# Splitting fp32 weight products into fp16 parts in the MLP and QKV projections of a fused transformer kernel

## The chip, the cores and the metric

The kernel runs on one core of a Trainium2 chip. Its time is the device time of one execution in microseconds (us). The engines are TensorE (PE in the profile, with PEld for its weight loads), VectorE (DVE), ScalarE (ACT), GpSimd (POOL) and SyncE (SP, which here only starts transfers).

## What is computed

A batch of 64 images of 224 x 224 with three channels (196 patches of 16 x 16) and 64 texts of 32 tokens. The sequence has 228 tokens of width 256. The reference, cut to what matters:

```python
patches = _patchify(x, 16)                              # 64 x 196 x 768
h = silu(patches @ tok_W1 + b1) @ tok_W2 + b2           # token projection
h = concatenate([h, txt], axis=1)                       # 64 x 228 x 256
# attention block on a = layernorm(h), 16 heads of 16
xn = rms_norm(a, ln1_w)
q, k, v = xn @ Wq, xn @ Wk, xn @ Wv                     # 256 x 256 each
q, k = q / |q|, k / |k|
p = softmax((q k^T + bias) * scale, earlier tokens only)
y = (p v) @ Wo + a
z = relu(rms_norm(y, ln2_w) @ W1) @ W2                  # 256 x 1024, 1024 x 256
h = h + z + y
# expert block on layernorm(h): 8 experts, each takes its best 3648 rows
scores = softmax(ln(h) @ Wr);  G, idx = top_k(scores.T, k)
X_e = gelu(X[idx] @ fW1 + fb1) @ fW2 + fb2
out = h + scatter_add(G * X_e)
```

## The kernel before

The kernel has two phases. In the first, 32 pairs of sequences (PAIRS, two sequences of 228 tokens, as four tiles of T = 114 rows, W = 456 columns when transposed) go through token projection, attention and MLP. The second does the routing and the experts; its products are already done in fp16 parts.

**Pipeline.** An iteration i of the first phase's loop does, on TensorE: the second token product of pair i (`pe_tok2`), the end of the attention of pair i-1, the router product of pair i-2 (`pe_x2T`, `pe_logits`), the output projection (`pe_yT`, `pe_wo`), the transposes of y (`pe_y2T`), and three up-projection blocks of pair i-1 (`pe_w1`; EARLY = 3 of MC = 8). Then come the transposes of pair i's normalised input (`pe_xsT`), one more block, the query, key and value products of pair i (`pe_qkv`, four query and key blocks and two value blocks), the last four up-projection blocks, and the attention of pair i (`pe_attention`). The down-projection of pair i-1 (`pe_w2`) is cut into 16 pieces of two products each: two pieces stand ahead of the transposed keys (`pe_qkT`), four between the first of them, and ten in numbered slots between the score and value products of the 16 groups of heads (`SLOTS`). The first token product of pair i+1 fills later slots. Iterations 1 to 30 are of this kind; the last (31) has no next token product, and a part "last" finishes the MLP of the last pair.

**Banks.** All products but the scores and the value products go through two PSUM banks, G[0] and G[1]. `BANKED`, `body` and `ORDER` write down by hand in which order blocks use each bank; a block may start when the one before it in its bank is evacuated (`wait_free`). All eight transposed query-key blocks use G[1].

**Other engines.** ScalarE evacuates the transposes (`act_evacuate`), the hidden blocks (`relu`), the queries and keys, and takes the exponentials (`exps`). VectorE does the layer norm and the normalised inputs xs and xa (`front_b`), the norms of queries and keys (`qk_norm`: a sum of squares for each of four tiles, a reciprocal root in 13 small steps, a scaling, and the fp16 low parts, after which the keys may be transposed), the multiplication with the bias table (`masked_probs`, 16 a pair), and the MLP output added to the residual (`mlp_out` after groups 1 and 6, `mlp_stats` after 7). POOL computes small norms, copies the high parts of queries, computes xn2 (`second_norm`), and reorders the images (`turn_images`), which SP then spreads over partitions (`spread_images`). Each engine works through its own list strictly in order.

**Start.** SP's queue loads the token weights and the images, spreads the first pair, loads the second, then the small weights; it writes the bias table to DRAM (`zrow_d`) when VectorE has made it, loads it back in eight transfers, then the attention and MLP weights, and only then spreads the second pair's images. POOL's list has the copy for the second pair's images ahead of the high parts of pair 0.

## Time and profile before

| | |
|---|---|
| median of 3 runs | 4300.19 us (4299.0 to 4302.61) |
| profiled execution | 4297.36 us, span 4295.6 us |
| granted TensorE clock, mean of the span | 0.968 |
| TensorE matmul busy | 3876.5 us, 90% |
| VectorE busy | 2403.7 us, 56% |
| ScalarE busy | 2035.7 us, 47% |
| GpSimd busy | 1716.9 us, 40% |

Busy shares are averages over both phases. In a timeline row a run of like instructions is merged: its start, its length, the engine, the line, the operation, output<-input, the shapes and the count, and in brackets how long the engine was idle before it and what ended that. Ends of matmuls include the time in which results drain, so the next row can start before the end of the one above. An fp32 product shows as two instructions.

### The profile page before, as it was taken

How to read it: one execution, taken by the hardware profiler on the slowest of the kernel's cores; microseconds unless marked ns; L12 is line 12 of the kernel's file. 1: busy time of each engine (PE TensorE's matmuls, PEld its weight loads, DVE VectorE, ACT ScalarE, POOL GpSimd, SP SyncE). 2: the span in 40 equal slices, each digit the busy share in tenths (PEclk: the TensorE clock that was granted, in tenths of full speed). 3: DMA queues.
4: the chain of work that ended last, by engine and by line, in shares of the span. 5: the costliest groups of instructions: out<-in, count | busy, mean ns of one | idle time of the engine just before them, and what ended most of it. 6: DMA issues, size and time to landing. Idle time of an engine off the chain costs nothing. (4 is left out here: it accounts for less than half of the span.)

```text
span 4295.6 us, 78024 instructions
## 1 busy us (share of the span) xinstructions
PE 3876.5 (90%) x26650; PEld 2354.5 (55%) x26650; DVE 2403.7 (56%) x4812; ACT 2035.7 (47%) x3375; POOL 1716.9 (40%) x1367
## 2 busy tenths in 40 slices
PE   2699999999999999999999999339999999999998
PEld 1366566566566566566566566235555555555554
DVE  3455555555555555555555555475555555555554
ACT  1344444444444444444444444225665655655565
POOL 1123323323323323323323322016666666666666
PEclk8799999999999999999999999659999999999999
DMA  7412312312312312312312310532323323323322
GB/s 113 87 35 43 49 34 44 49 34 44 49 34 44 49 34 44 49 34 44 49 34 44 49 22 16 143 99 39 63 45 66 63 46 65 65 46 66 46 46 45
DMA packets 302872, 222.26 MB, mean 52 GB/s; under 512 B 111524, under 2 KB 290182, under 8 KB 302710
## 3 DMA queue, kind: packets, MB, share of 16 engines
q1 hardware_dynamic: 183550, 157.86, 19.1%
q0 software_dynamic: 107264, 62.29, 9.3%
q10 hardware_dynamic: 11896, 0.05, 0.2%
q8 instruction: 89, 1.46, 0.1%
q14 instruction: 73, 0.60, 0.0%
HBM read 117.43 MB, written 63.57 MB: 42 GB/s over the span
## 5 line engine op out<-in xcount | busy, mean ns | idle before, releaser
L1382 DVE TENSOR_TENSOR pr<-pr,bias_t 114x684 f32<-114x684 f32 x512 | 485.6, 968 | 166.3 <-ACT pr L1018 161.9
L1729 POOL DMA_INDIRECT out_dram<-contrib,idx_cur x256 | 531.5, 2076 | 104.8 <-issue 78.8
L1558 DVE SCALAR_TENSOR_TENSOR hTs<-hTe,scales,hTs 128x456 f16<-128x456 f32 x514 | 322.4, 686 | 445.5 <-ACT hTs L1132 445.5
L1018 ACT ACTIVATE pr<-SC 114x684 f32<-114x684 f32 x512 | 376.5, 743 | 339.7 <-PE SC L445 339.4
L511 PE MATMUL G<-w2m,hT 128*114 128x256 f32 x2048 | 511.4, 388 | 1.1 <-DVE hy L1354 1.1
L891 PE MATMUL SC<-xgT,ws 128*128 128x456 f16 x2316 | 468.4, 357 | 0.0
L1722 POOL DMA_INDIRECT xg<-xn_rows,idx_cur x264 | 389.9, 1477 | 117.1 <-issue 60.4
L493 PE MATMUL G<-yT,w1m 128*128 128x456 f32 x1024 | 412.2, 551 | 10.6 <-ACT yT L964 10.6
L371 PE MATMUL G<-img,w1t 128*128 128x392 f32 x768 | 343.4, 538 | 68.3 <-DMA b2t<-in_L_tok_b_dram 49.9
L511 PEld LDWEIGHTS G<-w2m,hT 128*114 128x114 f32 x2048 | 339.9, 178 | 75.6 <-ACT hT L1054 15.4
L1660 POOL TENSOR_TENSOR rstd<-mv,ln_eps 114x4 f32<-114x4 f32 x32 | 7.0, 220 | 881.0 <-DVE mv L1255 881.0
L891 PEld LDWEIGHTS SC<-xgT,ws 128*128 128x128 f16 x2316 | 227.1, 98 | 220.3 <-issue 2.2
L1132 ACT ACTIVATE hTs<-hTe,scales 128x456 f16<-128x456 f32 x514 | 330.7, 670 | 0.0
L1125 ACT ACTIVATE hTe<-SC,fb1c,unscales 128x456 f32<-128x456 f32 x386 | 280.8, 728 | 54.4 <-PE SC L891 54.3
L902 PE MATMUL Y<-hTs,ws 128*128 128x456 f16 x1536 | 306.3, 356 | 0.0
L902 PE MATMUL SC<-hTs,ws 128*128 128x456 f16 x1536 | 306.3, 356 | 0.0
L493 PEld LDWEIGHTS G<-yT,w1m 128*128 128x128 f32 x1024 | 189.4, 190 | 180.5 <-issue 154.8
L1324 DVE COPY qkT<-G 128x912 f16<-128x912 f16 x128 | 81.0, 633 | 341.5 <-PE G L426 341.5
L1676 POOL CAST qkp<-qkraw 114x256 f16<-114x256 f32 x128 | 90.4, 744 | 444.6 <-DVE qkraw L1311 444.6
L1684 POOL COPY turned<-raw 96x1568 f32<-96x1568 f32 x64 | 203.3, 3176 | 114.6 <-DMA img<-turned 67.8
L1293 DVE TENSOR_TENSOR sqb<-qkraw 114x512 f32<-114x512 f32 x128 | 88.6, 692 | 277.9 <-ACT qkraw L964 277.9
L426 PE MATMUL G<-ident_h,qkp 114*128 114x114 f16 x2048 | 148.5, 216 | 93.5 <-POOL qkp L1676 48.7
(229 smaller groups left out, 6725.3 us busy)
## 6 DMA issues: line engine op xcount, KB each, us to landing
raw<-in_x_dram SPq DMA_DIRECT2D x192, 196.0 KB, 6.4
img<-turned SPq DMA_DIRECT2D x384, 98.0 KB, 2.8
we<-in_L_ffn_W_dram SPq DMA_DIRECT2D x34, 1024.0 KB, 7.7
out_dram<-hy SPq DMA_DIRECT2D x32, 456.0 KB
xn_rows<-xn SPq DMA_DIRECT2D x32, 456.0 KB
xg<-xn_rows,idx_cur POOLq DMA_INDIRECT x264, 3.8
out_dram<-contrib,idx_cur POOLq DMA_INDIRECT x256, 5.5
bias_by_distance<-pr SPq DMA_DIRECT2D x1, 3241.9 KB, 37.9
```

Source lines behind the costliest of these rows:

```text
L371: last = pe.matmul(part.g(*key)[:, 0:2 * NP_], w1t[:, k, m * 128:(m + 1) * 128], img[:, k, :, :].rearrange("p b n -> p (b n)"), start=k == ...
L493: last = pe.matmul(part.g("w1", m)[:, 0:W], w1m[:, c, m * 128:(m + 1) * 128], yT[:, c, :], start=c == 0, stop=c == KC - 1)
L511: last = pe.matmul(part.g("w2", b)[0:T, at:at + D], hT[:, m, t * T:(t + 1) * T], w2m[:, m, :], start=m == 0, stop=m == MC - 1)
L891: last = pe.matmul(RING[bank2(key)][:, 0:W], ws1[eb][:, wp, c, m * 128:(m + 1) * 128], xgT[:, xp, c, :], start=c == 0 and i == 0, stop=c = ...
L902: last = pe.matmul(RING[bank2(key)][:, 0:W], ws2[eb][:, wp, m, c * 128:(c + 1) * 128], hTs[:, hp, m, :], start=m == 0 and i == 0, stop=m = ...
L1018: act.activation(pr[g % 4][:, :, :], SC[g % 2][0:T, :, 0:QW], ACT.Exp).then_inc(exp_done, 1)
L1125: act.activation(hTe[:, m, :], RING[bank2(key)][:, 0:W], ACT.Gelu, bias=bias[:, at:at + 1] if isinstance(at, int) else bias[:, bass.ds(at, ...
L1132: act.activation(hTs[:, 0, m, :], hTe[:, m, :], ACT.Identity, scale=scale_at(scales, 2, e)).then_inc(h_high, 1)
L1382: dve.tensor_tensor(pr[g % 4][:, :, :], pr[g % 4][:, :, :], bias_t[:, 2 * pair:2 * pair + 2, :], ALU.mult).then_inc(probs_done, 1)
L1558: dve.scalar_tensor_tensor(hTs[:, 1, m, :], hTe[:, m, :], scale_at(scales, 2, e), hTs[:, 0, m, :], ALU.mult, ALU.subtract).then_inc(h_spli ...
L1722: pool.indirect_dma_start(out=xg[k4][:, t, :], out_offset=None, in_=xd[:, :], in_offset=bass.IndirectOffsetOnAxis(ap=idx_cur[k4][:, t:t + ...
L1729: pool.indirect_dma_start(out=out_rows, out_offset=bass.IndirectOffsetOnAxis(ap=idx_cur[k4][:, t:t + 1], axis=0), in_=contrib[k][:, t, :], ...
```

## The change

Six edits, all in the first phase.

- **Operands in two fp16 parts.** The weights of QKV, up- and down-projection are kept as a high part (rounded to fp16 after scaling by a power of two) and a low part (what is left); so are the transposed inputs and the hidden layer. A product becomes three fp16 products: high x high, high x low, low x high. `wo`, the token weights and the router stay fp32.
- **Evacuation in two passes.** ScalarE writes the high part from PSUM (`xs_high`, `y2_high`, `hid_high`); VectorE then reads the same PSUM block and the high part and writes the low part (`xs_low`, `y2_low`, `hid_low`); only then is the bank free. Evacuations of queries, keys and values take a scale.
- **Order.** All eight up-projection blocks stand ahead of QKV. Of the 16 down-projection pieces 12 stand ahead of the first transposed keys, two behind it, one each in slots 0 and 2. `mlp_out` for the first two tiles is moved into `qk_norm`, between the scaling and the low parts, the other two behind group 4, the statistics behind group 5.
- **Preparing weights.** The QKV weights are squared, scaled and split between the first token product and the first QKV (`qkv_split`); the MLP weights between the first attention and iteration 1 (`mlp_split_weights`). The raw weights lie in buffers that are used otherwise later.
- **Start.** The bias table waits for its own three small loads only and is written before the first images are spread, 341 columns instead of 455; it comes back in two transfers and one broadcast, and its subtraction stands before `qk_norm`. The expert biases are loaded on SP's queue after the second pair's images.
- **End.** For the last pair VectorE computes xn2 instead of POOL, and ScalarE does all eight hidden blocks.

```diff
-        wqkv = s1("wqkv", [128, KC, 3 * D])
+        wqkv = s1("wqkv", [128, 2, KC, 3 * D], F16)
-        w1m = s1("w1m", [128, KC, HID])
-        w2m = s1("w2m", [128, MC, D])
+        w1m = s1("w1m", [128, 2, KC, HID], F16)
+        w2m = s1("w2m", [128, 2, MC, D], F16)
...
         body = (
-            [("tok2", 0)] + BANKED["after"][0] + w1_blocks(0, 0, EARLY) + BANKED["front"][0] + BANKED["qkv"][0]
-            + w1_blocks(0, EARLY, MC) + [("w2", 0), ("w2", 1)],
+            [("tok2", 0)] + BANKED["after"][0] + w1_blocks(0, 0, EARLY) + BANKED["front"][0] + w1_blocks(0, EARLY, MC)
+            + BANKED["qkv"][0] + [("w2", 0), ("w2", 1)],
...
+        PARTS = ((0, 0), (0, 1), (1, 0))
...
                     for c in range(KC):
-                        last = pe.matmul(part.g(*key)[0:T, :], xsT[:, c, t * T:(t + 1) * T], wqkv[:, c, 0:2 * D],
-                                         start=c == 0, stop=c == KC - 1)
+                        for n, (wp, xp) in enumerate(PARTS):
+                            last = pe.matmul(part.g(*key)[0:T, :], xh[:, xp, c, t * T:(t + 1) * T], wqkv[:, wp, c, 0:2 * D],
+                                             start=c == 0 and n == 0, stop=c == KC - 1 and n == len(PARTS) - 1)
...
-                last = pe.matmul(part.g("w1", m)[:, 0:W], w1m[:, c, m * 128:(m + 1) * 128], yT[:, c, :],
-                                 start=c == 0, stop=c == KC - 1)
+                for n, (wp, yp) in enumerate(PARTS):
+                    last = pe.matmul(part.g("w1", m)[:, 0:W], w1m[:, wp, c, m * 128:(m + 1) * 128], yh[:, yp, c, :],
+                                     start=c == 0 and n == 0, stop=c == KC - 1 and n == len(PARTS) - 1)
...
-                    last = pe.matmul(part.g("w2", b)[0:T, at:at + D], hT[:, m, t * T:(t + 1) * T], w2m[:, m, :],
-                                     start=m == 0, stop=m == MC - 1)
+                    for i, (wp, hp) in enumerate(PARTS):
+                        last = pe.matmul(part.g("w2", b)[0:T, at:at + D], hT[:, hp, m, t * T:(t + 1) * T], w2m[:, wp, m, :],
+                                         start=m == 0 and i == 0, stop=m == MC - 1 and i == len(PARTS) - 1)
...
-        for n, slot in enumerate((0, 1, 4, 4, 5, 6, 7, 8, 9, 10)):
-            SLOTS[slot].append(("w2", range(6 + n, 7 + n)))
+        for n, slot in enumerate((0, 2)):
+            SLOTS[slot].append(("w2", range(14 + n, 15 + n)))
...
-            w2(0)
+            for n in range(0, 12, 2):
+                w2(n)
             pe_qkT(part, j, 0)
-            w2(2)
+            w2(12)
             pe_qkT(part, j, 1)
             pe_scores(part, j, 0, first)
-            w2(4)
             pe_scores(part, j, 1, first)
...
                 pe_xsT(part, i)
-                pe_w1(part, EARLY)
+                for m in range(EARLY, MC):
+                    pe_w1(part, m)
                 pe_qkv(part, i)
-                for m in range(EARLY + 1, MC):
-                    pe_w1(part, m)
                 pe_attention(part, i)
...
-                    act.activation(hT[:, m, :], part.g("w1", m)[:, 0:W], ACT.Relu).then_inc(evacuated[part.bank("w1", m)], 1)
+                    act.activation(hT[:, 0, m, :], part.g("w1", m)[:, 0:W], ACT.Relu).then_inc(hid_high, 1)
...
+            flat = lambda t: t.rearrange("p c n -> p (c n)")
+            squares_of(wo[:, :, :], yT[:, :, 0:D], WO_SUM, mlp_squares)
+            squares_of(flat(w1m_raw), words(w1m), W1_SUM, mlp_squares)
+            squares_of(flat(w2m_raw), words(w2m), W2_SUM, mlp_squares)
+            act.wait_ge(mlp_scale, 1)
+            high_weights(w1m[:, 0, :, :], w1m_raw, W1_K, mlp_high)
+            high_weights(w2m[:, 0, :, :], w2m_raw, W2_K, mlp_high)
...
                 xs_transposed(part)
-                relu(part, [EARLY])
+                relu(part, range(EARLY, MC))
                 queries_keys(part, i)
-                relu(part, range(EARLY + 1, MC - 2))
-                high_parts(i, range(3))
-                relu(part, [MC - 2])
-                high_parts(i, range(3, NT))
-                relu(part, [MC - 1])
+                high_parts(i, range(NT))
                 exps(part, i)
...
+            def hid_low(part, j, ms):
+                for m in ms:
+                    dve.wait_ge(hid_high, MC * j + (m + 1))
+                    dve.scalar_tensor_tensor(hT[:, 1, m, :], part.g("w1", m)[:, 0:W], 0.0, hT[:, 0, m, :],
+                                             ALU.max, ALU.subtract).then_inc(evacuated[part.bank("w1", m)], 1)
...
+                if part.kind != "first":
+                    mlp_out(part, j - 1, 0)
                 for t in range(NT):
                     dve.wait_ge(qk_high, NT * j + (t + 1))
...
                 router_out(i - 2)
-                front_b(part, i)
+                front_xs(i, range(2))
+                y2_low(part, i - 1)
+                front_xs(i, range(2, NT)).then_inc(xs_done, 1)
+                hid_low(part, i - 1, range(EARLY))
+                xs_low(part, i)
+                hid_low(part, i - 1, range(EARLY, MC))
+                front_xa(part, i)
                 qk_norm(part, i)
                 masked_probs(part, i)
```

## Rows read from the trace of the kernel before

**Rows 1.** The page's first part: busy time, share and instructions of each engine.

```profile
PE 3876.5 (90%) x26650; PEld 2354.5 (55%) x26650; DVE 2403.7 (56%) x4812; ACT 2035.7 (47%) x3375; POOL 1716.9 (40%) x1367
```

**Rows 2.** Windows: length; busy PE, PEld, DVE, ACT, POOL; PEclk; DMA share; GB/s.

```profile
64.10:66.80 2.70, 0.04 (x1) 0.00 (x0) 2.50 (x10) 0.00 (x0) 0.00 (x0) 1.00 0.92 98
67.00:72.00 5.00, 0.00 (x0) 0.00 (x0) 1.51 (x3) 0.00 (x0) 3.95 (x8) 0.50 0.94 99
...
137.00:148.70 11.70, 8.55 (x88) 5.98 (x89) 3.70 (x5) 5.68 (x8) 0.00 (x0) 0.50 1.00 139
149.00:155.50 6.50, 3.87 (x58) 2.27 (x55) 5.00 (x5) 3.66 (x6) 2.86 (x1) 1.00 0.31 35
155.80:159.00 3.20, 3.20 (x30) 1.50 (x28) 1.40 (x2) 0.00 (x0) 0.00 (x0) 0.50 0.00 0
...
1464.40:1545.00 80.60, 76.74 (x569) 48.26 (x569) 46.90 (x100) 36.36 (x63) 24.22 (x24) 1.00 0.24 42
...
2656.00:2667.50 11.50, 6.96 (x153) 4.83 (x153) 9.42 (x20) 6.22 (x11) 9.08 (x6) 1.00 0.14 43
```

**Rows 3.** Timeline of PE over one body iteration.

```profile
1464.42 1.95 PE L389 MATMUL G<-w2t,hid 128*114 128x256 f32 x8
...
1476.66 1.00 PE L360 MATMUL G<-ident,yn 114*128 114x114 f32 x8 [0.78 <-DVE yn L1372]
...
1485.52 7.03 PE L406 MATMUL G<-wqkv,xsT 128*114 128x512 f32 x16
...
1495.84 6.28 PE L493 MATMUL G<-yT,w1m 128*128 128x456 f32 x16
1501.96 1.91 PE L511 MATMUL G<-w2m,hT 128*114 128x256 f32 x8
1505.28 0.57 PE L426 MATMUL G<-ident_h,qkp 114*128 114x114 f16 x8 [1.42 <-DVE qkp L1319]
...
1545.00 1.95 PE L389 MATMUL G<-w2t,hid 128*114 128x256 f32 x8
```

**Rows 4.** Timelines of ACT and DVE in the same iteration.

```profile
1481.32 0.55 ACT L1054 ACTIVATE hT<-G 128x456 f32<-128x456 f32 x1 [0.98 <-PE G L493]
...
1478.86 1.37 DVE L1286 TENSOR_SCALAR xa<-h,mv,lt 114x256 f32<-114x256 f32 x4
...
1494.65 0.23 DVE L1301 TENSOR_SCALAR ss<-ss 114x128 f32<-114x128 f32 x1
...
1498.63 2.90 DVE L1311 TENSOR_TENSOR qkraw<-qkraw,rn 114x512 f32<-114x512 f32 x4
1501.45 1.15 DVE L1318 TENSOR_TENSOR qkp<-qkraw,qkp 114x256 f16<-114x256 f32 x2
```

**Rows 5.** Groups of instructions: busy us, mean ns of one, idle before, releaser.

```profile
L1558 DVE SCALAR_TENSOR_TENSOR hTs<-hTe,scales,hTs 128x456 f16<-128x456 f32 x514 | 322.4, 686 | 445.5 <-ACT hTs L1132 445.5
...
L1293 DVE TENSOR_TENSOR sqb<-qkraw 114x512 f32<-114x512 f32 x128 | 88.6, 692 | 277.9 <-ACT qkraw L964 277.9
...
L1354 DVE SCALAR_TENSOR_TENSOR hy<-G,r,hy 114x256 f32<-114x256 f32 x128 | 55.6, 476 | 13.7 <-PE G L511 13.7
...
L1112 ACT ACTIVATE hTe<-we 128x2048 f32<-128x2048 f32 x16 | 30.6, 1910 | 47.1 <-DMA we<-in_L_ffn_W_dram 46.8
```

**Rows 6.** Timeline of PE in the expert phase, a dense fp16 run.

```profile
3508.24 4.79 PE L902 MATMUL SC<-hTs,ws 128*128 128x456 f16 x24
```

**Rows 7.** Timeline of PE, attention of the first pair (no down-projection in it).

```profile
137.08 0.92 PE L426 MATMUL G<-ident_h,qkp 114*128 114x114 f16 x8 [48.70 <-POOL qkp L1676]
...
149.91 0.31 PE L443 MATMUL SC<-qkT 64*114 64x228 f16 x2 [0.72 <-DVE qkT L1324]
...
153.38 0.31 PE L443 MATMUL SC<-qkT 64*114 64x228 f16 x2 [0.73 <-DVE qkT L1324]
...
161.07 0.58 PE L461 MATMUL Y<-pr,v 114*17 114x228 f32 x8
```

**Rows 8.** Timeline of POOL behind the last pair's statistics.

```profile
2710.94 4.84 POOL L1663 TENSOR_SCALAR xn<-hy,mv,rstd 114x256 f32<-114x256 f32 x4
```

More of the change, by code:

```diff
@@ L1099, in _ @@
             squares(part)
-            relu(part, range(4))
+            relu(part, range(MC))
             x2_transposed(PAIRS - 1)
@@ L1420, in _ @@
             router_out(j - 1)
-            relu(part, range(4, MC))
+            y2_low(part, j)
+            hid_low(part, j, range(MC))
             mlp_out(part, j, 0)
```

237 lines of the change are left out of this document (168 added, 69 removed).

## The prediction

> **What bounds the kernel now.** I read the page's first part before anything else: TensorE is busy for 90% of the span [rows 1], so the question is in which stretches that share is real work. The timeline of TensorE then shows the body iteration, which is most of the span: the second token-projection block starts at 1464.42 us in one iteration and at 1545.00 in the next, a period of 80.58 us, 30 times over [rows 3]. The windows view of that period has TensorE busy 76.7 us, VectorE 46.9, ScalarE 36.4, at the full clock throughout [rows 2]. So before, the body is bound by TensorE, with only some 4 us of waits in it, and every TensorE instruction that is taken out would shorten it, as long as the others keep up.
>
> The reader should cut the iteration in four [rows 3]: the front (1464.42 to 1476.66: token projection, output projection, router), the up-projection and the query, key and value (QKV) projections (1476.66 to 1501.96), the first down-projection pieces and a wait of 1.42 us for the keys (to 1505.28), and the attention with 14 of 16 down-projection pieces strewn in as filler (to 1545.00, 39.7 us).
>
> **The arithmetic on TensorE.** Three fp16 products take the place of one fp32 product of two instructions. A dense run of 24 fp16 products of 456 columns takes 4.79 us at the full clock, start to start 0.193 us each [rows 6], which is one column per cycle at 2.4 GHz. For 256 and 512 columns I scale by columns: 0.109 and 0.215 us. The bounds are the eight 114-column transposes in 0.57 us (71 ns each with the drain, [rows 3]), scaled up 0.16 us for 256, and the pure column rate, 0.107; I take the dense run, because these are dense runs too.
> - Up-projection, 8 blocks: 1.16 us each of work instead of 1.53 (the last four blocks stand from 1495.84 to 1501.96, [rows 3]). Saving 3.0 us.
> - QKV: four query and key blocks of 6 x 0.215 = 1.29 us and two value blocks of 12 x 0.109 = 1.31, 7.8 us instead of 10.32 (1485.52 to 1495.84, [rows 3]). Saving 2.5 us.
> - Down-projection, 16 pieces: 6 x 0.109 = 0.65 us instead of 0.955 (two pieces in 1.91, [rows 3]). Saving 4.8 us.
> Together 10.3 us per iteration, if TensorE stays the bound. I think that it does not, for three reasons, each with its place.
>
> **First place: the up-projection's banks.** Its blocks go through two PSUM banks. Before, a block was freed by one ScalarE pass of 0.55 us [rows 4]. Now ScalarE writes the high part (0.55) and VectorE then the low part, PSUM and fp16 to fp16. The nearest row is the expert phase's low part of the same shape and form, 0.686 us on average and 322.4 / 514 = 0.627 of its own time [rows 5]. Its first source lies in SBUF where the new one lies in PSUM; I take 0.69 (bounds 0.63 and 0.75). A bank then turns in 1.16 + 0.2 + 0.55 + 0.03 + 0.69 + 0.13 (the three waits read off the gaps between engines) = 2.76 us, 1.4 per block. Blocks 0 to 2, the two transposed halves of the next input, which now also need two passes, and blocks 3 to 7, written out one after the other, put the first query product at 1476.66 + 15.1, where the same work took 8.86 + 6.12 = 15.0 before. The 3.0 us are gone: +0.1.
>
> **Second place: the wait for the keys.** QKV takes 7.9 us and the 12 pieces of down-projection now put ahead of the keys 7.9 us: 15.8 us of cover after the last up-projection block. Behind it VectorE has: its last low part (over 1.3 us after QKV starts), the four xa passes of 1.37 us [rows 4], four sums of squares at 1.45 us (two passes of 0.69 and their waits, [rows 5]) = 5.8, the reciprocal root 4.0 (1494.65 to 1498.63), the scaling 2.9, the moved output pass of two tiles 0.9 (0.476 each, [rows 5]), and the key and query low parts 3.3 [rows 4]. That is 1.3 + 1.4 + 5.8 + 4.0 + 2.9 + 0.9 + 3.3 = 19.6 us against 15.8. So TensorE stands about 3.7 us at the keys instead of 1.42. Bounds: 2.5 (low parts at 0.63, every overlap used) and 5.
>
> **Third place: attention without its filler.** 39.7 us less 14 pieces of 0.955 is 26.3, plus 4 pieces of 0.65 that stay is 28.9. But the transposed keys go through a single bank: transpose, evacuation by ScalarE or VectorE in turn, scores, next transpose. The first pair's attention, which has no down-projection in it, shows what that chain takes at the full clock: its scores start at 149.91 and two groups later at 153.38, 3.5 us for two groups [rows 7], of which TensorE works 2.2. Over the eight blocks the last evacuation ends 14.1 us after the first transposes, against 9.5 us of work that TensorE has until then (8 x 0.42 transposes, 7 x 0.29 scores, 4 x 0.65 down-projection, 2 x 0.74 value products): 4.6 us of waits. VectorE's second output pass and statistics (2.7 us), moved to groups 4 and 5, hold the third group of value products for another 0.5, about what today's attention loses in the same place. Bounds 3 and 6. Attention at the full clock: 33.5 us.
>
> Sum at the full clock: 12.2 + 15.1 + 7.9 + 7.9 + 3.7 + 33.5 = 80.3 us against 80.6. All of the 10.3 us is given back as waits.
>
> **The clock.** TensorE's granted clock follows how busy it has been. In this trace it was 1.00 while TensorE worked to 64.1 us and through the first 2.7 us of the wait after, and 0.50 from 67.0 on; it was 0.50 for the first 11.7 us of the first pair's attention, 1.00 in the next 6.5 us, in which TensorE was busy 60%, then 0.50 again (the stretch at 155.8); the last pair's attention, 61% busy from 2656.0 to 2667.5, ended in the same fall [rows 2]. In the body it is 1.00, because the waits are short. After the change each iteration has a wait of 3.7 us, and behind it the thinnest stretch of all, like the first pair's. I expect a fall to 1.2 GHz near the keys in nearly every iteration, and a second one after the thin stretch in some 4 of 10. Cost: from the keys to the second scores TensorE has 2.3 us of work, which doubles, then the four pieces soon bring the clock back: +2.3 on average. The second fall halves the clock over dense work for as long as at 155.8 to 159.0, 3.2 us [rows 2], +1.6, times 0.4: +0.6. With some chance that the low clock stays longer, I take +3.3. Bounds per iteration: 0 (no fall), and +5.6 (the first pair needed 24.0 us from its keys (137.08) to its fourth group of value products (161.07, [rows 7]), where I count 19.4 for the body at the full clock, and it has neither the four pieces nor the two VectorE steps, another 1.0).
> The Trainium skill says the same of such loops ("TensorE: Matmul & The Clock Gate", section "HAM oscillation — how this bites in real kernels"): a kernel whose TensorE waits between bursts in each iteration is put back to half rate each time, and pays for it each time. By that rule the change ends slower; by the sum at the full clock alone it would end 0.5% faster.
>
> **Start and end.** Before, the first pair's keys wait 48.70 us, for the copy on POOL [rows 7]; POOL is behind the second pair's images, and those on SP's queue behind the bias table and the weights. After: the table goes out before the first images (token work some 11 us later), three loads in place of eight, and the 10 small loads leave the front of ScalarE's queue. The keys should come at about 118 us instead of 137. What is given back: between the first attention and the second pair stand three sums of squares on ScalarE (1.91 us for 2048 columns, [rows 5], 4.7 in all), a product (0.5), sixteen small VectorE steps of 0.25 (4.0), one high part (1.9) and two low parts of 2048 columns (four times 0.6 each, 4.8), one behind the other: 15.9 us with TensorE idle. Net -3 us (bounds -15 and +12: what loads on one queue cost each other is not shown). At the end, the last pair's 16 pieces save 4.8, the row norm moves from POOL (4.84 us, [rows 8]) to VectorE (four passes, 1.4 us), -3.4, and the last pair's attention, all filler before, gives by the same chain about -4: -12 us. The expert phase is untouched; its small bias loads moved to SP's queue land long before.
>
> **Sum.** 30 x (80.3 - 80.6 + 3.3) = +90, -3, -12: +75 us. The profiled execution took 4297.4 us (span 4295.6), 2.8 below the median of the runs; so 4300.2 + 75 = about 4375 us, slower by 1.7%.
>
> **Rivals.**
> - The clock holds. For: the 1.42 us wait of today costs no clock, and the down-projection ahead of the keys is dense. Against: rows 2, and a wait more than twice as long. 30 x (-0.3) - 15 = -24: 4276 us, faster by 0.6%. It decides the sign: below 0.8 us of clock cost per iteration the change is not slower. Chance 0.2.
> - VectorE's chain is shorter than I add up, and TensorE stays the bound: the waits at the keys stay under 2 us and the clock is up, so that half to all of the 10.3 us stays. For: VectorE is busy only 46.9 us of 80.6 and gets some 7.5 more. Against: it is the chain's length and not the sum that counts. From 30 x (-5) - 15 to 30 x (-10) - 15: 3980 to 4135 us. Chance 0.12.
> - The low clock stays through the thin stretch in each iteration, as at the first pair: 30 x (-0.3 + 5.6) - 15 = +144, 4444 us. Chance 0.15.
> - My forecast, a fall in most iterations that costs 1.2 to 4.5 us in each: 30 x 0.9 - 15 to 30 x 4.2 - 15, so 4312 to 4411 us. Chance 0.5; the rest, 0.03, lies outside all.
>
> 0.2% is about what a measurement of this kernel can tell from no change. Within it: 0.07, from the low end of the forecast and the high end of the first rival. Faster 0.32, slower 0.61. The range reaches from below the first rival (4276, less 30 x 1.7 if the wait for the keys is at its lower bound and half a microsecond more is won elsewhere: 4225) to the third, 4450; the forecast's own is 4312 to 4411.
>
> **What would show it.** Right: a body period of 82 to 85 us; a wait of 3 to 5 us before the transposed keys, released by VectorE's key parts; up-projection blocks about 1.4 us apart, each waiting for VectorE; the granted clock at 0.50 for some us at the start of each attention. Wrong: a wait at the keys under 2 us, or the clock at 1.00 in the whole body, or a low part of the hidden layer far from 0.69 us; then the period says which rival it is. The first keys should come at 110 to 126 us, and a gap of 13 to 19 us should stand behind the first attention.

## The result, and the profile after

The changed kernel takes 4335.12 us (median of 4 runs, 4332.87 to 4337.33) against 4299.59 us (4297.12 to 4302.61) for the kernel before in the same session: ratio 1.0082, 95% interval 1.0065 to 1.0100. It is slower by 0.8%. The forecast was slower by 1.7%.

The busy line of the page, to be laid beside [rows 1]:

```profile
PE 3688.2 (85%) x28702; PEld 2353.2 (54%) x28702; DVE 2632.2 (61%) x5223; ACT 2084.5 (48%) x3393; POOL 1744.1 (40%) x1395
```

TensorE has 188 us less work and VectorE 229 more. The windows view cuts the span at four events: the second pair's iteration, the 29 iterations up to the last pair's, what lies up to the transposes of the router's scores, and the rest (columns as in [rows 2]). After:

```profile
161.47:255.27 93.80, 77.89 (x634) 53.73 (x634) 60.80 (x130) 40.85 (x64) 25.98 (x26) 0.90 0.18 31
255.27:2631.15 2375.88, 2039.91 (x18329) 1390.26 (x18329) 1554.74 (x3248) 1084.53 (x1798) 724.83 (x724) 0.98 0.24 41
2631.15:2763.72 132.57, 99.95 (x841) 73.54 (x841) 74.02 (x163) 46.15 (x85) 24.77 (x30) 0.87 0.09 30
2763.72:4335.50 1571.78, 1410.26 (x8450) 799.18 (x8450) 876.77 (x1522) 868.24 (x1391) 945.92 (x586) 0.94 0.34 63
```

The same windows of the kernel before:

```profile
175.21:255.78 80.57, 76.73 (x568) 48.24 (x569) 47.16 (x100) 36.33 (x63) 24.13 (x24) 1.00 0.26 44
255.78:2592.38 2336.60, 2225.38 (x16472) 1399.18 (x16473) 1358.60 (x2900) 1053.68 (x1798) 699.04 (x695) 1.00 0.24 42
2592.38:2729.83 137.45, 108.95 (x728) 75.76 (x728) 61.89 (x141) 42.67 (x81) 29.85 (x32) 0.91 0.09 28
2729.83:4295.60 1565.77, 1405.63 (x8450) 797.32 (x8450) 875.95 (x1522) 868.37 (x1391) 941.82 (x586) 0.94 0.34 63
```

The span is 39.9 us longer (4335.5 against 4295.6), and 39.3 of them lie in the second row: 29 iterations of 81.93 us on average instead of 80.57. The start gains 13.7 us up to the second pair and gives 13.2 back in its iteration. The end of the first phase gains 4.9, and the last row loses 6.0 in code that the change leaves alone. That last row isn't the change's doing: it took from 1561.1 to 1576.2 us in the profiled executions of the experiments below.

Before, every iteration took 80.57 us. After, they repeat in a pattern of six, of which four are shown. The last three columns are granted clock, DMA share and GB/s:

```profile
1238.24:1318.89 80.65, 68.65 (x633) 46.28 (x633) 53.65 (x112) 37.37 (x63) 25.11 (x25) 1.00 0.24 42
1318.89:1401.53 82.64, 71.26 (x633) 48.87 (x633) 53.62 (x112) 37.47 (x63) 25.11 (x25) 0.96 0.23 41
1401.53:1484.77 83.24, 71.69 (x633) 48.57 (x633) 53.74 (x112) 37.48 (x63) 25.11 (x25) 0.96 0.23 41
1484.77:1566.43 81.66, 70.13 (x632) 48.01 (x633) 53.66 (x112) 37.35 (x63) 25.13 (x25) 0.98 0.24 42
```

The first row is the key to the result: at the full clock the iteration takes 80.65 us, what it took before. The mean is 1.28 us longer, over 29 iterations 37 us, and that is the whole loss: without the low clock the changed kernel would take some 4298 us (an estimate from these rows). TensorE is busy 68.65 us of it instead of 76.74 [rows 2], and idle 12.0 instead of 3.8. Its timeline in that iteration answers to [rows 3]:

```profile
1250.48 1.00 PE L388 MATMUL G<-ident,yn 114*128 114x114 f32 x8 [0.78 <-DVE yn L1480]
1252.86 2.47 PE L527 MATMUL G<-yT,w1m 128*128 128x456 f16 x12 [1.39 <-DVE yT L1393]
...
1258.12 0.61 PE L388 MATMUL G<-ident,xs 114*128 114x114 f32 x4 [0.87 <-DVE hT L1399]
1258.67 6.61 PE L527 MATMUL G<-yT,w1m 128*128 128x456 f16 x30
1265.32 5.39 PE L435 MATMUL G<-wqkv,xsT 128*114 128x512 f16 x24
...
1273.16 5.40 PE L546 MATMUL G<-w2m,hT 128*114 128x256 f16 x48
1281.50 2.83 PE L546 MATMUL G<-w2m,hT 128*114 128x256 f16 x24 [2.94 <-DVE stage L1462]
1284.80 0.57 PE L457 MATMUL G<-ident_h,qkp 114*128 114x114 f16 x8 [0.47 <-DVE qkp L1433]
```

Front 12.24 us, up-projection with the next input 14.84, QKV 7.84, twelve down-projection pieces and their waits 11.64, attention 34.09. The large wait, 2.94 us, isn't at the keys. It is at the ninth piece, which opens the second half of the down-projection in the same bank: that bank is free only when VectorE has made the moved output pass (L1462). VectorE's timeline behind its last low part of the hidden values:

```profile
1265.89 0.63 DVE L1399 SCALAR_TENSOR_TENSOR hT<-G,hT 128x456 f16<-128x456 f32 x1 [0.63 <-ACT hT L1095]
1266.44 1.37 DVE L1380 TENSOR_SCALAR xa<-h,mv,lt 114x256 f32<-114x256 f32 x4
...
1277.77 2.89 DVE L1423 TENSOR_TENSOR qkraw<-qkraw,rn 114x512 f32<-114x512 f32 x4
1280.58 0.86 DVE L1462 SCALAR_TENSOR_TENSOR stage<-G,r,stage 114x256 f32<-114x256 f32 x2
...
1284.46 0.21 DVE L1433 COPY qkp<-qkp 114x256 f16<-114x256 f16 x1
```

Behind its first row none has an idle time ahead: from 1265.89 to 1284.67 VectorE goes from step to step (the xa passes, the sums of squares, the root, the scaling, the output pass, the low parts), and TensorE waits twice for it.

What the clock does, in windows of the fourth iteration (the wait, the four pieces behind it, the rest), of the third (the wait at the up-projection, then its first blocks) and of the second (53 us into it, early in the attention):

```profile
1525.10:1528.00 2.90, 0.00 (x0) 0.00 (x0) 2.90 (x6) 2.37 (x4) 2.67 (x4) 1.00 0.00 0
1529.00:1532.30 3.30, 3.30 (x18) 3.30 (x17) 2.19 (x9) 0.00 (x0) 0.00 (x0) 0.51 0.00 0
1532.50:1566.40 33.90, 28.74 (x377) 17.56 (x374) 20.89 (x34) 20.13 (x27) 11.66 (x7) 1.00 0.09 28
1411.50:1416.00 4.50, 2.48 (x15) 1.68 (x13) 3.46 (x7) 1.59 (x5) 3.54 (x4) 1.00 0.00 0
1416.50:1419.50 3.00, 3.00 (x9) 1.18 (x8) 1.05 (x4) 1.22 (x5) 2.10 (x4) 0.50 0.00 0
1371.70:1375.20 3.50, 3.36 (x26) 2.63 (x27) 2.01 (x4) 1.39 (x3) 0.00 (x0) 0.52 0.00 0
```

In the fourth iteration the clock is 1.00 through the wait, falls when dense work has begun again, and is back before the attention, which then runs at 2.4 GHz throughout. So it is in five of six iterations, except that in two of them the low clock reaches up to 0.8 us into the attention. The second has a further fall inside the attention: from the keys to the end of the iteration it takes 35.35 us there, and 34.09 at the full clock.

### The profile page after: what moved, and what is told of

Same layout as the page of the kernel before. It is cut to its first block and busy times, and to the rows that moved or that the text cites. A ratio compares the mean times of both kernels' runs of the same rounds, so it can differ in the third digit from the quotient of the medians.

```text
span 4335.5 us, 82911 instructions
## 1 busy us (share of the span) xinstructions
PE 3688.2 (85%) x28702; PEld 2353.2 (54%) x28702; DVE 2632.2 (61%) x5223; ACT 2084.5 (48%) x3393; POOL 1744.1 (40%) x1395
## 5 line engine op out<-in xcount | busy, mean ns | idle before, releaser
L1490 DVE TENSOR_TENSOR pr<-pr,bias_t 114x684 f32<-114x684 f32 x512 | 475.8, 962 | 160.6 <-ACT pr L1057 159.5
L546 PE MATMUL G<-w2m,hT 128*114 128x256 f16 x3072 | 405.6, 293 | 91.6 <-DVE stage L1462 91.6
L546 PEld LDWEIGHTS G<-w2m,hT 128*114 128x114 f16 x3072 | 372.1, 142 | 99.8 <-DVE stage L1462 99.5
L527 PE MATMUL G<-yT,w1m 128*128 128x456 f16 x1536 | 337.6, 365 | 53.9 <-DVE yT L1393 44.6
L1784 POOL TENSOR_TENSOR rstd<-mv,ln_eps 114x4 f32<-114x4 f32 x32 | 22.9, 717 | 718.0 <-DVE mv L1348 718.0
L1399 DVE SCALAR_TENSOR_TENSOR hT<-G,hT 128x456 f16<-128x456 f32 x256 | 161.9, 632 | 188.9 <-ACT hT L1095 188.9
L474 PE MATMUL SC<-qkT 64*114 64x228 f16 x1024 | 161.2, 308 | 126.0 <-ACT qkT L1018 56.5
L527 PEld LDWEIGHTS G<-yT,w1m 128*128 128x128 f16 x1536 | 134.9, 99 | 240.1 <-DVE hT L1399 57.7
L1018 ACT COPY qkT<-G 128x912 f16<-128x912 f16 x128 | 117.3, 917 | 249.1 <-PE G L457 249.1
```

Of the source, the lines that this page charges most:

```text
L527: last = pe.matmul(part.g("w1", m)[:, 0:W], w1m[:, wp, c, m * 128:(m + 1) * 128], yh[:, yp, c, :], start=c == 0 and n == 0, stop=c == KC - ...
L546: last = pe.matmul(part.g("w2", b)[0:T, at:at + D], hT[:, hp, m, t * T:(t + 1) * T], w2m[:, wp, m, :], start=m == 0 and i == 0, stop=m == ...
L1490: dve.tensor_tensor(pr[g % 4][:, :, :], pr[g % 4][:, :, :], bias_t[:, 2 * pair:2 * pair + 2, :], ALU.mult).then_inc(probs_done, 1)
```

## The experiments

Times are medians. "Mean" is the mean of the 29 iterations between the third and the last pair, "full clock" an iteration at 1.00 where the trace has one. The ratios are to the kernel before in the same session, whose median lay between 4297.3 and 4304.5 us.

| run | us | ratio to before (95%) | mean | full clock |
|---|---|---|---|---|
| before | 4299.59 | | 80.57 | 80.57 |
| changed | 4335.12 | 1.0082 (1.0065 to 1.0100) | 81.93 | 80.65 |
| 1 fill at the ninth piece | 4325.03 | 1.0057 (1.0041 to 1.0074) | 81.43 | 80.64 |
| 2 fp32, changed order | 4406.70 | 1.0253 (1.0235 to 1.0271) | 83.91 | 83.71 |
| 3 fp16, order back | 4282.40 | 0.9956 (0.9939 to 0.9972) | 80.17 | none |
| 4 changed, 8 pieces ahead | 4390.31 | 1.0208 (1.0191 to 1.0225) | 83.59 | none |
| 5 run 3 with fill | 4234.71 | 0.9850 (0.9833 to 0.9866) | 78.76 | 78.65 |
| 6 QKV alone, order before | 4274.02 | 0.9943 (0.9925 to 0.9962) | 80.40 | 80.39 |
| 7 QKV and up-projection | 4304.29 | 1.0014 (1.0004 to 1.0023) | 81.31 | none |
| 8 run 7, pieces moved up | 4530.22 | 1.0539 (1.0522 to 1.0557) | 88.58 | none |
| 9 run 7, ReLUs first | 4315.70 | 1.0032 (1.0018 to 1.0046) | 81.40 | none |
| 10 run 9 with fill | 4268.54 | 0.9929 (0.9912 to 0.9945) | 79.87 | 79.00 |
| 11 changed, fill in both waits | 4323.19 | 1.0058 (1.0035 to 1.0081) | 81.62 | 80.68 |
| 12 changed, one Newton step | 4265.18 | 0.9925 (0.9908 to 0.9941) | 79.62 | 78.68 |
| 13 run 5, one Newton step | 4268.26 | 0.9917 (0.9901 to 0.9934) | 79.92 | 78.20 |

The theory behind the first four: the order gives the saving back, not the arithmetic, and the clock takes some more. The rival: VectorE's low parts cost what they save, whatever the order.

**Run 1, work in the wait at the ninth piece.**

```diff
             for n in range(0, 8, 2):
                 w2(n)
+            if not first:
+                for _ in range(24):
+                    pe.matmul(SC[0][0:T, 0, 0:D], hT[:, 0, 0, 0:T], w2m[:, 0, 0, :], start=True, stop=True)
             for n in range(8, 12, 2):
                 w2(n)
```

> The changed kernel with 24 added products of 256 columns (into a score bank that nobody reads) between the eighth and the ninth down-projection piece, where TensorE waits 2.93 us for the moved mlp_out; output is unaffected. Theory (the clock falls in the dense pieces follow from that idle stretch and cost about 1 us in most iterations): the falls about 44.5 us into the iteration vanish, period 81.93 to about 80.9, time 4335 to about 4305 (4295 to 4320). Rival (the falls have nothing to do with this wait, or come elsewhere instead): period 81.7 to 82.3 and 4330 to 4345, or more if the 24 products outlast the wait.

```profile
1149.45:1230.09 80.64, 71.26 (x656) 48.89 (x657) 53.66 (x112) 37.34 (x63) 25.09 (x25) 1.00 0.24 42
1230.09:1312.23 82.14, 72.73 (x656) 49.35 (x657) 53.77 (x112) 37.50 (x63) 25.11 (x25) 0.98 0.24 42
```

The falls behind that wait are gone, as the theory says, but in half of the iterations one stands at the start of the up-projection (14.5 us in), where the changed kernel had it in one of six. It costs 1.3 to 1.5 us. So the mean iteration came to 81.43 us where 80.9 was expected, and the time fell by 10 us and not by 30.

**Run 2, the order alone.** The kernel before, with the changed kernel's order:

```diff
-            w2(0)
+            for n in range(0, 12, 2):
+                w2(n)
             pe_qkT(part, j, 0)
-            w2(2)
+            w2(12)
...
-                pe_w1(part, EARLY)
-                pe_qkv(part, i)
-                for m in range(EARLY + 1, MC):
+                for m in range(EARLY, MC):
                     pe_w1(part, m)
+                pe_qkv(part, i)
```

and likewise in the bank lists, the slots, ScalarE's queue and the place of `mlp_out`.

> The kernel before, fp32 products and its own start, with only the changed kernel's order: all eight up-projection blocks ahead of the query, key and value projections, twelve down-projection pieces ahead of the keys, mlp_out(0) before the keys' low parts, two filler pieces in the attention. Theory (the order is what gives the saving back): period 82.5 to 84.5 against 80.57, time about 4390 (4360 to 4420). Rival (the order is free and the fp16 arithmetic's low parts cost the time): period 80.6 +- 0.5, time 4290 to 4315.

```profile
845.21:928.92 83.71, 76.53 (x568) 49.02 (x569) 46.41 (x100) 36.49 (x63) 25.08 (x24) 1.00 0.24 41
```

TensorE does the same work and stands 7.18 us instead of 3.84. The order costs 3.1 us an iteration, and the rival of a free order is out. These waits aren't those of the changed kernel: at the ninth piece TensorE waits 0.97 us and at the keys not at all, and 3.6 us lie ahead of scores in the attention, which has lost its filler.

**Run 3, fp16 with the order back**, eight pieces ahead of the keys, eight as filler, the last low parts of the hidden values between and behind the Newton steps:

```diff
             for n in range(0, 8, 2):
                 w2(n)
             pe_qkT(part, j, 0)
             pe_qkT(part, j, 1)
...
+                    if part.kind != "first" and n < 2:
+                        hid_low(part, j - 1, [EARLY + 1 + n])
```

> The changed kernel's fp16 arithmetic and start with nearly the order of before: three blocks, the front, one block, the projections, four blocks; eight down-projection pieces ahead of the keys and eight as filler in the attention; mlp_out(0) behind the keys' low parts. Theory (the order gives the saving back): most of the 10.3 us per iteration comes through where VectorE's chain runs beside the last up-projection blocks, period 76 to 78, time about 4165 (4130 to 4220). Rival (VectorE's added low parts, 5.5 us an iteration, are the cost whatever the order): period 80.5 or more, time 4295 or more.

```profile
1213.06:1291.99 78.93, 69.93 (x632) 47.30 (x633) 53.71 (x112) 37.50 (x63) 25.45 (x25) 0.98 0.25 43
1291.99:1373.51 81.52, 72.73 (x633) 48.57 (x633) 53.81 (x112) 37.67 (x63) 25.45 (x25) 0.94 0.25 42
```

Faster than before, but by 0.4% and not by 3%: neither theory had the size. Every iteration has a fall, every second one three times as much low clock. The first row's one fall, early in the attention, costs only 0.28 us against the full-clock iteration of the same order in run 5 (78.65).

**Run 4, the changed kernel with eight pieces ahead of the keys**, `mlp_out(0)` behind the keys' low parts, the other eight as filler.

> The changed kernel with only eight pieces ahead of the keys, the other eight as filler in the attention, and mlp_out(0) behind the keys' low parts, so that no piece waits for it. Theory (piece 9's wait for mlp_out is on the path, and VectorE's chain sets the keys): keys start about 0.9 us earlier after the first piece, one wait of about 5 us ahead of them, attention 34 to 36 us, clock falls as before or more; period 81.0 to 82.5, time 4310 to 4350. Rival (the filler hides wholly in the attention's waits and the clock holds): period about 80 and 4280 or less.

```profile
1130.00:1135.80 5.80, 0.00 (x0) 0.00 (x0) 5.80 (x16) 2.37 (x4) 2.86 (x4) 0.74 0.00 0
1133.00:1143.00 10.00, 5.76 (x45) 4.28 (x46) 5.00 (x15) 4.53 (x6) 0.00 (x0) 0.50 0.00 0
```

Two short waits became one of 5.84 us at the keys. The clock falls half way through it and is then low for 10.2 us, where it was low for 3.4 in the changed kernel. Whether the longer wait does that, or the thin work behind it (short products with waits between them), isn't separated. In every second iteration there is a fall of 3.4 us at the up-projection besides. The expectation had the wait and missed this; the time came out 40 us above its upper end.

What the low clock costs there can be read beside run 5, which has the same work in the same order from the keys to the end of the iteration (and eight added products in a wait between the first two keys), but at the full clock. First run 4, then run 5:

```profile
1135.84:1172.21 36.37, 34.00 (x400) 21.85 (x401) 21.48 (x36) 20.30 (x28) 11.82 (x7) 0.90 0.08 26
```

```profile
1159.63:1194.79 35.16, 32.49 (x408) 20.87 (x409) 21.55 (x36) 20.19 (x28) 11.82 (x7) 1.00 0.09 27
1165.16 0.31 PE L474 MATMUL SC<-qkT 64*114 64x228 f16 x2 [1.13 <-ACT qkT L1025]
```

The cost is 1.2 us, and 1.8 in the other iterations of run 4 (36.95). It is less than the doubled work, because part of that falls into waits: the wait of 1.13 us for a transposed key in run 5 isn't there in run 4.

**Run 5, run 3 with added products in its waits**: 12 behind the y2T transposes, 14 ahead of the first keys, 8 between the first two.

```diff
+        def fill(n):
+            for _ in range(n):
+                pe.matmul(SC[0][0:T, 0, 0:D], wqkv[:, 0, 0, 0:T], wqkv[:, 0, 0, 0:D], start=True, stop=True)
```

> The third experiment's kernel (fp16 arithmetic, nearly the order of before) with added products of 256 columns in its waits: 12 behind the y2T transposes (wait 1.39 us), 14 ahead of the first keys (1.76 us) and 8 between the first two (1.01 us); output unaffected. Theory (each clock fall of 3.4 us costs about 1.3 us of the period and follows these waits; without falls the period of this order is about 77.6): falls mostly gone, period 77.6 to 78.7, time 4205 to 4240. Rival (the falls stay or move elsewhere in the attention): period 79.5 or more, 4260 or more.

```profile
1116.14:1194.79 78.65, 72.22 (x666) 49.77 (x667) 53.73 (x112) 37.40 (x63) 25.48 (x25) 1.00 0.25 43
```

The added products ahead of the keys don't delay them (43.49 us into the iteration, 43.47 in run 3). The clock holds in 27 of 29 iterations, and the kernel is 1.5% faster than before and 2.3% faster than the changed one: 1.4 us an iteration for 34 products that compute nothing. It is the best of all runs here.

**Run 6, only QKV split**, all else of the MLP as before, no split of its weights.

> Only the query, key and value products split to fp16, the MLP's in fp32, in the order of before; start of the changed kernel without the MLP weights' split. Theory (the projections' split costs VectorE only its 1.3 us of low parts, and most of its 2.5 us come through): period 78.5 to 79.8 against 80.57, and the start about 14 us earlier: 4225 to 4265. Rival (the wait for the keys takes it all back, since VectorE's sums set them): period about 80.5, 4275 to 4290.

```profile
PE G L460 <- DVE qkp L1425: 1.4, 1, 1.4
PE G L547 <- ACT hT L1093: 1.4, 1, 1.4
...
PE G L529 <- DVE xsT L1381: 0.5, 1, 0.5
```

These are TensorE's waits in one iteration (total, times, longest). The rival was right: 2.5 us saved, 0.18 left. The wait for the keys is 1.4 as before, and 1.4 stand newly ahead of the first down-projection piece, for ScalarE's last ReLU, and 0.5 for the input's low part. The gain of this run is its start: its third pair begins at 235.37 us and before at 255.78. So the start edits without the MLP weights' split are worth 20.4 us. The changed kernel gives 19.9 of them back by its third pair: by that split, and by some 0.3 to 1.5 us that its second pair's iteration takes longer in the new order (by the means and full-clock figures above).

**Run 7, QKV and up-projection in fp16, down-projection in fp32**, so that a hidden block needs one ReLU pass and no low part.

> Projections and up-projection in fp16, down-projection in fp32 with a single ReLU pass per block on ScalarE (no low part of the hidden values), in the order of before. Theory (the hidden values' low parts, eight of 0.63 us on VectorE in the bank's cycle and in its chain, give back most of the MLP's saving): period 76 to 78.5, time 4180 to 4250. Rival (the saving of the up-projection is lost to the keys' wait whatever the evacuation): no faster than the kernel with the projections alone, 4250 or more.

TensorE, and ScalarE beside it:

```profile
1411.61 4.78 PE L530 MATMUL G<-yT,w1m 128*128 128x456 f16 x24
1419.31 3.63 PE L548 MATMUL G<-w2m,hT 128*114 128x256 f32 x8 [2.92 <-ACT hT L1100]
```

```profile
1416.79 1.22 ACT L1053 CAST qkp<-qkraw 114x512 f16<-114x512 f32 x2 [2.11 <-DVE qkraw L1427]
...
1418.72 0.54 ACT L1100 ACTIVATE hT<-G 128x456 f32<-128x456 f32 x1
```

Blocks 4 to 7 now run without a gap (1.2 us each), so the low parts' cycle is gone. But the seventh ReLU (1418.72) stands in ScalarE's queue behind copies that wait for VectorE's scaled queries, and the first piece waits 2.92 us for its bank. The expectation (4180 to 4250) overlooked that queue: an order that fitted the slower blocks doesn't fit the faster ones.

**Runs 8 to 10.** Run 8 moves pieces 2 and 3 ahead of the keys without touching that queue. Runs 9 and 10 put all ReLUs ahead of the copies; run 10 adds the 12 products behind the y2T transposes.

```diff
-                relu(part, range(EARLY + 1, MC - 2))
-                high_parts(i, range(3))
-                relu(part, [MC - 2])
-                high_parts(i, range(3, NT))
-                relu(part, [MC - 1])
+                relu(part, range(EARLY + 1, MC))
+                high_parts(i, range(NT))
```

> As the run with projections and up-projection in fp16, with down-projection pieces 2 and 3 ahead of the first keys instead of behind them, and each later pair moved up likewise. Theory (VectorE's chain sets the keys' start, and real work fits in ahead of them at no cost): 0.5 to 1.4 us an iteration less than that run, so 15 to 40 us. Rival (the keys then wait on TensorE, or the attention lacks the filler): no change within 5 us, or slower.

> Projections and up-projection in fp16, down-projection in fp32, order of before, but ScalarE's last four ReLUs stand ahead of the four copies that make the keys' high parts, and pieces 2 and 3 stand ahead of the first keys. Theory (the wait of 2.92 us of the first piece is ScalarE's in-order queue: ReLU 6 and 7 stand behind copies that wait for VectorE's root; VectorE then sets the keys at about 19.5 us behind the first projection either way, and two fp32 pieces fit ahead of them): keys at the same place, attention about 2.7 us shorter, clock falls fewer; period 75.5 to 77.5, time 4165 to 4235. Rival (the copies, now behind the ReLUs, delay the keys by as much): period 78.5 or more, 4250 or more.

> The same with 12 added products of 256 columns behind the y2T transposes, in the wait for y2_low (1.39 us). Theory (that wait brings about the clock fall of 3.4 us at the start of the up-projection in part of the iterations): the falls about 15 us into the iteration vanish, 0.4 to 1.3 us less an iteration. Rival (no such falls are left in this order, or they move): within 5 us of the run without them.

Run 8 kept the 2.9 us wait, got one of 2.3 for `mlp_out(0)` (its ninth piece stood in an earlier slot than that pass), and fell into the low clock three times an iteration, mean 0.90. It is 226 us slower than run 7; its rival allowed for slower, but neither had that size, and it wasn't followed up. Run 9 lost the wait for the ReLU and found it at the keys:

```profile
PE G L460 <- DVE qkp L1432: 2.8, 1, 2.8
```

The number is the rival's (81.40 us an iteration, 4316 us), its reason is not: the keys start 18.8 us behind the first projection, as in run 7 (19.0), and the copies don't hold them. VectorE's chain does, and with less work ahead of the keys TensorE waits for it there. In run 10 the falls 15 us in are gone, as its theory says, and many of those 40 us in as well, so it gains 47 us, more than the 0.4 to 1.3 us an iteration expected. Its full-clock iteration of 79.00 and that of run 5, 78.65, are close; that splitting the down-projection too (run 5) costs and saves about the same is likely, but the two also differ in order, so it isn't shown.

**Run 11, the changed kernel with both waits filled.**

> The changed kernel with added products in both of its waits: the 24 between the eighth and the ninth down-projection piece and 12 behind the y2T transposes. Theory (with the clock held, the fp16 products in this order are worth nothing against before: iteration 80.65 as in the full-clock iterations): no falls in the body, period 80.65, time 4293 to 4305. Rival (a fall moves elsewhere, as the second one did when the first wait was filled): period 81.0 or more, 4308 or more.

```profile
336.04:416.72 80.68, 72.58 (x669) 50.19 (x669) 53.66 (x112) 37.41 (x63) 25.17 (x25) 1.00 0.24 42
1148.99:1230.90 81.91, 74.00 (x668) 51.32 (x669) 53.64 (x112) 37.49 (x63) 25.14 (x25) 0.98 0.23 42
```

The full-clock length is confirmed at 80.68, but from the seventh iteration on nearly all (22 of 29) have a fall 52 us in, in the thin start of the attention, where the changed kernel had one in one of six and run 1 none: the rival. Filling a wait removed the fall behind it, and falls came elsewhere.

**Run 12, a shorter chain on VectorE.** The reciprocal root is refined in three Newton steps of three dependent instructions each; two steps are left out.

```diff
-                for _ in range(3):
+                for _ in range(1):
                     step(dve.tensor_tensor(a_, r_, r_, ALU.mult))
```

> The changed kernel with one Newton step instead of three in VectorE's root for the query and key norms (two steps are left out, so the norms are less exact), which takes six dependent instructions, about 1.9 us, out of VectorE's chain and nothing off TensorE. Theory (VectorE's chain from the last hidden low part through the sums, the root and mlp_out sets when the ninth piece and the keys run): the 2.93 us wait shrinks to about 1.0, the iteration by 1.9 us at full clock (80.65 to about 78.8) and more where the fall behind that wait goes with it: time 4265 to 4285. Rival (TensorE or the attention sets the period and the wait is only where slack collects): period 81.5 to 82, 4325 or more.

```profile
1206.80:1285.48 78.68, 68.66 (x632) 46.27 (x633) 51.90 (x106) 37.36 (x63) 25.12 (x25) 1.00 0.26 43
```

Nothing was taken off TensorE (68.66 us busy, as in the changed kernel), 1.97 us off VectorE's chain, and the iteration is 1.97 us shorter; the wait at the ninth piece is 1.0 us. That is the direct proof that VectorE's chain sets the period in the changed order at the full clock. (The mean fell by more, from 81.93 to 79.62, since the falls behind that wait went too; one stands 50 us in or 15 us in, in two of three iterations.)

**Run 13, the same in the order of run 3.**

> The fifth experiment's kernel (fp16 arithmetic, nearly the order of before, added products in the waits) with one Newton step instead of three (two are left out, so the norms are less exact) and without the 14 added products ahead of the keys. Theory (in this order too VectorE's root stands in the way of the keys at its full length): keys and period 1.9 us earlier, 78.64 to about 76.7, time 4180 or less. Rival (here the low parts of hidden blocks 4 to 7, each a cycle of block, ReLU and low part in one bank, end as late as the root, and set the scaling's start): 0.3 to 1.0 us, period 77.6 to 78.3, time 4205 to 4225.

```profile
1005.38 0.63 DVE L1406 SCALAR_TENSOR_TENSOR hT<-G,hT 128x456 f16<-128x456 f32 x1 [1.18 <-ACT hT L1101]
1006.53 0.63 DVE L1406 SCALAR_TENSOR_TENSOR hT<-G,hT 128x456 f16<-128x456 f32 x1 [0.52 <-ACT hT L1101]
1007.08 2.89 DVE L1434 TENSOR_TENSOR qkraw<-qkraw,rn 114x512 f32<-114x512 f32 x4
```

0.45 us at the full clock (78.65 to 78.20), the rival; with the falls the mean is 79.92 and the time 43 us above the rival's upper end. VectorE now idles 1.18 and 0.52 us for the ReLUs of the last two blocks, and its scaling starts only behind their low parts: here the bank cycle of blocks 4 to 7 holds the keys. Without the 14 products ahead of the keys the falls came back, and the run is slower than run 5.

## Why the forecast had the direction and twice the size

The two orders and the two arithmetics, iterations at the full clock:

| | order before | changed order |
|---|---|---|
| fp32 | 80.57 | 83.71 |
| fp16 | 78.65 (run 5) | 80.65 |

The arithmetic is worth 1.9 us in the one order and 3.1 in the other, of nearly 10 that it takes off TensorE; the new order costs 3.1 or 2.0. The two cancel. (Run 5 places pieces and low parts its own way, so the lower left figure is that order as nearly as it could be had.)

- **TensorE's products.** Right. Up-projection 1.16 to 1.2 us a block, QKV 7.84 (forecast 7.9), pieces 0.67 each (0.65): some 9.8 us saved where 10.3 were counted (8.1 by busy time, 76.74 - 68.65, in which the drain of each separate run counts).
- **First place, the banks.** Right in the sum, 14.84 us against 15.1, less so in its parts: the low part is 0.63 us and not 0.69, blocks 3 to 7 run at 1.3 us, and 1.39 us stand at the first block for the low part of its input, which I had not put there. The group of the new pass, to be laid beside [rows 5], and the low part of y, of the same form and shape:

```profile
L1399 DVE SCALAR_TENSOR_TENSOR hT<-G,hT 128x456 f16<-128x456 f32 x256 | 161.9, 632 | 188.9 <-ACT hT L1095 188.9
L1393 DVE SCALAR_TENSOR_TENSOR yT<-G,w_scale,yT 128x456 f16<-128x456 f32 x64 | 41.0, 678 | 1.3 <-ACT yT L1089 1.3
```

  The expert row that I took (686 ns; nearly every pass of it takes 680 to 700) was another pass in more than its source. It reads its scalar from a tile (`scales`), and the hidden layer's low part has a constant. The second line reads PSUM like the first, but its scalar from a tile (`w_scale`), and takes 678 ns: so the source isn't what made most of the difference. (The first operation differs as well, a maximum against a product; the two weren't separated.)
  The Trainium skill ("VectorE: DVE Perf Modes", section "The TRN2 errata — SBUF-src ops pay a fixed extra latency per instruction") gives for an fp32 `tensor_tensor` add the elements plus 151, over 0.96 GHz. Taken over to this pass, which is of another form and reads PSUM, that gives an estimate of 632 ns for 456 elements. The trace agrees with 632 for the pass with the constant, and not for the one with the tile (678).
- **Second place, the wait at the keys.** Right in size: chain 19.35 us from the first projection (forecast 19.6), waits 2.94 + 0.47 = 3.41 us (forecast 3.7). Wrong in place: I let all twelve pieces run as cover, but the ninth needs the bank that the moved `mlp_out(0)` empties. That moved the clock's fall as well, see below. That the wait is VectorE's chain is shown by run 12.
- **Third place, the attention.** 34.09 us against 33.5. Right.
- **Sum at the full clock.** 80.65 against 80.3.
- **The clock: the step that failed, by its size.** Forecast +3.3 us an iteration, measured 81.93 - 80.65 = 1.28; over 29 iterations that is 59 us too much, more than the whole miss. How often was right: the falls came in five of six iterations, a second one in two of six (I had 4 in 10). Where and at what price was not. I had the fall at the keys, with thin work behind it, at 2.3 us; since the wait stands at the ninth piece, it came over the four dense pieces instead and costs 1.0 us, and the attention, TensorE busy 85% of it, ran at the full clock in five of six iterations (but for up to 0.8 us at its start). The second fall costs 1.6 us at the up-projection and 1.3 in the attention (forecast 1.6). The price would have been too high at the keys as well: in run 4 the clock is low there for 10.2 us, and that costs 1.2 to 1.8 us. I doubled TensorE's work and let all of it count, where part of it falls into waits for the transposed keys. The +5.6 of the upper bound was read from the first pair's attention, and no iteration came near it: the longest is 2.6 us over the full-clock one.
  The Trainium skill ("TensorE: Matmul & The Clock Gate", section "HAM oscillation — how this bites in real kernels") has the loop throttled in every round because of its waits, and cures it by keeping the engine in work. This case agrees with the cure in run 5 and not in run 11, where both waits are filled and 22 of 29 iterations still have a fall. The changed kernel's trace agrees only in part with the rule: one iteration in six has the same wait of 2.9 us and no fall, and a fall in another stands behind a wait of 1.39.
- **Start.** Net -0.5 us against -3: first keys at 114.75 us (forecast 118), edits worth 20.4 (19), given back 19.9 (15.9). The split's chain is as long as I added it up, 15.0 us from 156.37 to 171.39, but TensorE isn't idle through it: it stands 5.19 us, works on the second pair's token products, and stands 3.75 us behind them. So the sign that I named, a gap of 13 to 19 us, didn't show. The low clock has a part in the rest: the second pair's iteration has it at 0.90 on average.
- **End.** Forecast -12, measured 132.57 - 137.45 = -4.9 up to the router's scores, and then 6.0 lost in a phase that varies by 15 between executions. The missing 7 us weren't followed up. Part of them can be the clock: by the windows above it was low for some 34 of the 132.57 us, and before for some 25 of the 137.45.

By terms: +11 at the full clock, -59 for the clock, +3 at the start, +13 at the end, and -3 because 29 periods lie between those marks and not 30: -35, where the spans differ by 39.9 instead of 75. The clock's error is larger than the miss; the others, nearly all of the other sign, took 24 us of it back, which is luck. The direction is not luck: the body is level at the full clock, as forecast, and the low clock makes it slower.

Of the rivals, "the clock holds" (4276) wasn't reached, not even with both waits filled (run 11, 4323). A low clock through the whole thin stretch (4444) is out: five of six iterations have at most 0.8 us of it in the attention, the sixth 3.4 us. TensorE as the bound is out by run 12.

Open: what decides whether a fall comes in one iteration and not in the next, with the same instructions and the same waits, and why filling one wait moves falls to another place. Also whether run 5's gain can be had by real work in place of the added products; that was not tried in its order (run 8 tried it in that of run 7, and lost).

## What to carry to other kernels

Take time off the busiest engine only after following the chain of the next one: here nearly 10 us off TensorE were worth 2 to 3, and 2 us off VectorE's chain were worth 2. When blocks get faster, look again at every in-order queue that was laid out for the slower ones (ScalarE's ReLUs in run 7), and at who empties the bank that a moved piece needs. A wait of 1 to 3 us in a loop can have a second price, the clock. A fall of 3.4 us cost 0.3 to 1.6 us of an iteration here, and dense work behind the wait was no cheaper than thin. Don't count the work at 1.2 GHz twice without looking for waits that take part of it up. Filling the waits paid in one order (run 5) and hardly in the other (runs 1 and 11), so it has to be tried.

## What the runs showed of the hardware

- A wait of 2.94 us with dense fp16 products behind it went with 3.4 us at 1.2 GHz, at a price of 1.0 us. One of 5.84 us with thin work behind it (run 4) went with 10.2 us, which began half way through the wait, at a price of 1.2 to 1.8 us.
- One fall of 3.4 us in the attention cost 0.3 us (run 3), 1.2 (run 11), 1.3 (run 12, the changed kernel) or 1.6 (run 5).
- A VectorE pass with a constant as its scalar took 632 ns for 456 elements from PSUM; one of the same form and shape with its scalar in a tile took 678 ns.
- A fall stood behind a wait of only 1.39 us, in thin surroundings (TensorE busy 2.48 of 4.50 us before it).
- Products that nobody reads, 34 of 256 columns in each iteration's waits, raised the mean granted clock from 0.943 (run 3) to 0.966 (run 5) and took 48 us off.
- Iterations of identical instructions fell into patterns of two (run 3), three (run 12), five (run 7) or six iterations (the changed kernel), each repeated to a few hundredths of a microsecond.
